# Graph attention edge stages: four buffers of turned one-hots, a ring of ten messages, rounds of turned one-hots and scores at other tiles, both scans for the highest score together

## The reference

```python
xp = (x @ W).reshape(-1, Hh, C)
alpha = a_src[src] + a_dst[dst] + a_edge
alpha = leaky_relu(alpha, 0.2)
m = segment_max(alpha, dst)
ex = exp(alpha - m[dst])
denom = segment_sum(ex, dst)
alpha = ex / (denom[dst] + 1e-16)
out = segment_sum(xp[src] * alpha[:, :, None], dst) + bias
```

## Time and profile before

| what | us |
|---|---|
| median of 3 runs | 3561.06 (3548.32 to 3565.73) |
| profiled execution, its own time | 3566.32 |
| its span, first to last instruction | 3564.4 |
| both edge stages with the join between them | about 140 to 3230 of the span |

### The profile page before, as it was taken

How to read it: one execution, slowest core, us unless ns; L and a number is a source line. 1 busy time by engine, 2 the same in 40 slices (tenths; PEclk the granted TensorE clock), 3 DMA queues, 4 the chain that set the end, 5 groups by cost and what they waited for, 6 DMA issues and landing times. The chain is left out here.

```text
span 3564.4 us, 57920 instructions
## 1 busy us (share of the span) xinstructions
PE 2549.3 (72%) x15613; PEld 2149.2 (60%) x15614; DVE 2146.7 (60%) x6378; ACT 1130.1 (32%) x3915; POOL 2046.6 (57%) x2269
## 2 busy tenths in 40 slices
PE   5376876777777777764777676767676766859897
PEld 4265655655666565644666666656566664648786
DVE  6265666666666665634666665656666666676565
ACT  3133333333333333441222222222222223532222
POOL 3465665565656565365565565656566553636665
PEclk9677777777777777786677776777777767969999
DMA  9544544444444444134444444544444442554443
GB/s 238 168 136 124 139 127 131 132 130 132 133 134 134 132 134 133 50 113 121 136 138 138 137 139 127 146 127 141 134 141 136 138 124 74 166 146 153 141 120 93
DMA packets 282383, 475.56 MB, mean 133 GB/s; under 512 B 69124, under 2 KB 191644, under 8 KB 282116
## 3 DMA queue, kind: packets, MB, share of 16 engines
q0 software_dynamic: 96912, 288.68, 29.9%
q1 hardware_dynamic: 120884, 137.12, 12.5%
q10 hardware_dynamic: 64320, 46.56, 4.2%
HBM read 398.47 MB, written 75.78 MB: 133 GB/s over the span
## 5 line engine op out<-in xcount | busy, mean ns | idle before, releaser
L708 POOL DMA_INDIRECT e_rows<-table,e_idx x1664 | 1610.0, 968 | 1091.9 <-DVE e_msg L749 665.1
L1094 PE MATMUL e_ps_sum<-e_hot,e_msg 128*128 128x128 f32 x6656 | 1196.5, 339 | 251.4 <-DVE e_msg L749 139.4
L1094 PEld LDWEIGHTS e_ps_sum<-e_hot,e_msg 128*128 128x128 f32 x6656 | 1058.0, 242 | 309.0 <-DVE e_msg L749 173.8
L946 ACT ACTIVATE acc<-e_ps_sum 128x256 f32 x1664 | 641.8, 386 | 1574.3 <-remote 929.3
L749 DVE TENSOR_TENSOR e_msg<-e_rows,e_ps_pr 128x256 f32<-128x256 f32 x1664 | 672.2, 416 | 40.3 <-PE e_ps_pr L1085 11.3
L1074 PE MATMUL e_ps_al<-e_dst_score,e_hotT 128*128 x3328 | 331.3, 186 | 376.5 <-issue 209.9
L1074 PEld LDWEIGHTS e_ps_al<-e_dst_score,e_hotT 128*128 128x128 bf16 x3328 | 258.0, 104 | 522.4 <-issue 452.5
L738 DVE TENSOR_SCALAR e_hotT<-e_relb,pcolf 128x512 bf16<-128x512 bf16 x416 | 147.6, 355 | 495.5 <-remote 380.6
L724 DVE TENSOR_TENSOR e_hot<-e_ps_pr,rel 128x508 f32<-128x508 f32 x416 | 283.5, 682 | 0.0
L767 DVE TENSOR_TENSOR e_al<-e_ps_al,e_rows 128x128 f32<-128x128 f32 x104 | 30.3, 292 | 381.5 <-remote 201.4
L2292 ACT ACTIVATE x_h<-x,eb 128x128 f32<-128x128 f32 x216 | 67.9, 366 | 277.9 <-PE x L2366 229.7
(11 more groups left out here) (370 smaller groups left out, 3562.8 us busy)
## 6 DMA issues: line engine op xcount, KB each, us to landing
e_relb<-rel_rows SPq DMA_DIRECT2D x104, 512.0 KB
e_rows<-table,e_idx POOLq DMA_INDIRECT x1664
e_eattr<-in_edge_b SPq DMA_DIRECT2D x104, 128.0 KB
e_xT<-turned_x ACTq DMA_DIRECT2D x100, 128.0 KB
e_xr<-in_x ACTq DMA_DIRECT2D x100, 128.0 KB
node<-l_row SPq DMA_DIRECT2D x25, 512.0 KB, 3.2
table<-t_row SPq DMA_DIRECT2D x25, 276.0 KB
table<-j_row SPq DMA_DIRECT2D x25, 276.0 KB, 2.5
```

The costliest lines, as they stand in the source:

```text
L708: nc.gpsimd.indirect_dma_start(out=rows[q][:, k, :], out_offset=None, in_=table[0:NP], in_offset=bass.IndirectOffsetOnAxis(ap=idx[:, q, k: ...
L946: nc.scalar.activation(acc[:, :, bass.ds(at[k + e], P)], ps_sum[pair % 3][:, e], ACT.Copy).then_inc(s["window"], 1)
L1094: op = nc.tensor.matmul(ps_sum[pair % 3][:, e, a], msg[:, (16 * g + k + e) % RM, a * P:a * P + P], hot[:, (4 * g + k // 4) % RH, (k + e) % ...
```

## The change

`e_hotT` gets four buffers, one for each round, so a round now waits only for the same round of the group before (for r = 3, the `scores` of the group before). The ring of messages shrinks from 14 slots to 10, which frees the same 4 KB of a partition: a message at even k now waits for the pair five back, not seven. DVE makes the rounds at k = 2, 3, 6, 14, and PE uses them at k = 9, 10, 11, 14. `highest` moves from k = 7 to k = 8, straight ahead of `less_highest`.

```diff
-    RM = 14
+    RM = 10
-        hotT = tmp("hotT", [P, 2, 2, 4, P], BF16)
+        hotT = tmp("hotT", [P, 4, 2, 4, P], BF16)
...
                 if r == 0:
                     vec.wait_ge(s[f"rel{q}"], 16 * i + 16)
-                    if g > 0:
-                        vec.wait_ge(s["part"], 3 * g)
-                elif r == 1:
-                    vec.wait_ge(s["scores"], g + 2)
-                else:
-                    vec.wait_ge(s["part"], 3 * g + r - 1)
+                if g > 0:
+                    if r < 3:
+                        vec.wait_ge(s["part"], 3 * g - 2 + r)
+                    else:
+                        vec.wait_ge(s["scores"], g + 2)
...
-                    if ahead and k in (3, 6, 14, 15):
-                        turned_hots(g + 2, q, {3: 0, 6: 1, 14: 2, 15: 3}[k], i + 1)
+                    if ahead and k in (2, 3, 6, 14):
+                        turned_hots(g + 2, q, {2: 0, 3: 1, 6: 2, 14: 3}[k], i + 1)
...
-                    if softmax and k == 7:
+                    if softmax and k == 8:
                         highest(n, p, i if p == 1 else i + 1)
-                    if softmax and k == 8:
                         less_highest(n, p)
...
-                    if ahead and k in (9, 10, 14, 15):
-                        scores(m, q, {9: 0, 10: 1, 14: 2, 15: 3}[k], j)
+                    if ahead and k in (9, 10, 11, 14):
+                        scores(m, q, {9: 0, 10: 1, 11: 2, 14: 3}[k], j)
```

More of the change, by code:

```diff
@@ L730, in turned_hots @@
                     vec.wait_ge(s[f"rel{q}"], 16 * i + 16)
-                    if g > 0:
-                        vec.wait_ge(s["part"], 3 * g)
-                elif r == 1:
-                    vec.wait_ge(s["scores"], g + 2)
-                else:
-                    vec.wait_ge(s["part"], 3 * g + r - 1)
+                if g > 0:
[3 more added lines that the diff above has]
+                        vec.wait_ge(s["scores"], g + 2)
                 for far, number in enumerate((v["pcolf"], v["pfar"])):
-                    op = nc.vector.tensor_scalar(hotT[:, r % 2, far], relb[:, q, 4 * r:4 * r + 4, :], number[:, 0:1], None,
+                    op = nc.vector.tensor_scalar(hotT[:, r, far], relb[:, q, 4 * r:4 * r + 4, :], number[:, 0:1], None,
                                                  ALU.is_equal)
@@ L1073, in scores @@
                     for far in range(2):
-                        op = nc.tensor.matmul(parts_al[:, m, :], hotT[:, r % 2, far, k, :],
+                        op = nc.tensor.matmul(parts_al[:, m, :], hotT[:, r, far, k, :],
                                               pieces[:, bass.ds(b + far, 1), :].rearrange("p a c -> p (a c)"), start=False,
```

## The result

The changed kernel takes 3592.14 us (median of 4 runs, 3585.7 to 3596.23), beside 3558.88 us for the kernel before in the same comparison. The ratio is 1.0094, with a 95% interval of 1.0065 to 1.0124: slower, by about 33 us. Four executions agree within 11 us, so the sign is clear of noise. I had forecast 3522 us and faster. The time is inside the range of 3415 to 3630 us, the direction is wrong.

What follows compares the result with a forecast made beforehand. No engine is full; waits going round between engines, followed through POOL's two gaps, set the time. Per step 0.54 us gained, 0 for gap two, 0.13 lost: 0.41 us, times 100 steps 41 us, so 3522 us; range 3415 to 3630 us.

Steps and rivals of the forecast that it cites:

- The wait on this group's `part` goes, and the stall moves to message 0.: DVE at k = 14 no longer waits; it waits for `probT` at the next step's k = 0, one gather later.
- signs that I had named: One-hots' idle time (about 496 us) nearly gone, `e_msg` idle 300 us or more, `leaky` clearly under 381.5, POOL's waiting about 620.
- wrong, to the bad: Signs of a slower kernel: idle time ahead of `e_peak`, or POOL waiting over 700 us for messages.
- Gap one becomes 1.71 + 0.68 = 2.39 us instead of 2.93.: POOL's stop ahead of DVE's third round: release plus POOL's lag, no round between; 0.54 us less a step.
- I take no change: POOL's stop behind `leaky` keeps its 1.78 us; bounds were all of 1.48 us won and 1.89 us more.
- gap two: POOL's second stop in a step, waiting for the message behind DVE's `leaky`: 1.78 us before the change.
- the scans stand behind a stall: Rival: `turned` comes late, both scans and the subtraction delay message 9; 1.48 us a step slower, 3709 us; chance 0.18.
- Ring of ten: 0.: Message 14 waits for its own group's third pair instead of the first; expected cost 0.
- the ring of ten binds: Rival: DVE stops at k = 14, PE at the sixth pair, a third gap; 0.9 us a step, 3650 us; chance 0.08.
- Rounds inside a run: 0.13 us lost.: DVE's round 2 moves into POOL's run of gathers, lengthening one gather from 0.95 to 1.08 us each step.
- PE's late news is tied to POOL's run, as I read it: All PE signals are held back while POOL gathers back to back, arriving 1.71 us after its run stops.

Runs made afterwards that it cites:

- B: The measuring condition of those comparisons in which the unchanged kernel before takes about 2995 us.
- A: The measuring condition of those comparisons in which the unchanged kernel before takes about 3560 to 3590 us.
- g1: Changed kernel with SP's fetch also waiting for `leaky` of the group two back, on A: 3671.46 us, 1.0243 of the kernel before.
- i1: Changed kernel with SP's fetch also waiting for `leaky` of the group two back, on B: 2971.87 us, 0.9928 of the kernel before.

## Why the prediction was wrong

The time was foreseen as 41 us less and came out as 33 us more. Point by point:

- *The wait on this group's `part` goes, and the stall moves to message 0.* Right, and so were the signs that I had named: 4.1 us ahead of L737, 521.4 us ahead of the messages, and a `leaky` that hardly waits. My signs of "wrong, to the bad" were met too: idle time ahead of `e_peak`, and 728.1 us of POOL's waiting.
- *"Gap one becomes 1.71 + 0.68 = 2.39 us instead of 2.93."* This term failed, and is the larger error: 0.78 us a step between the forecast and the mean of the layers. The place lost 0.01 us in layer 0 and gained 0.48 in layer 1, on average +0.24 instead of -0.54. Of the two addends, the release was met in the step shown (1.67 us), but over 105 waits its mean is 1.90 us (ahead of messages, those over 6 us left out). The other addend I took from the wrong place: POOL starts 1.17 us behind message 0, not 0.68 us as behind messages 15 and 5. I could have read this in the trace of before, where the lag of the first gather of a group has the same mean, 1.2 us. What fills the extra half us no row shows. So the half us that I won by taking a round out of the stall (0.54 us) was lost again, which accounts for a gap that keeps its size. The 0.48 us by which it grew in layer 1 lie at k = 14, where the ring of ten waits. My base was also one short step: 24.92 us, where the mean of the kernel before is 25.7 us in layer 0 and 25.9 us in layer 1.
- *"I take no change"* for gap two. This step failed. It grew by 0.85 us a step in layer 0 and fell by 0.28 us in layer 1, on average +0.29. The mechanism is that of my rival *the scans stand behind a stall*: DVE reached the scans in the silent part of POOL's run in 74 steps, and stood there for 346.6 us. I gave it 0.18 and priced it at 1.89 us for each step. It was met in three steps of four and cost less than that, since the gap in front of it (k = 5, 1.47 and 1.10 us a step before) vanished at the same time. In layer 1 a wait that I didn't count came in front of it, that of `mixed` (64.9 us). I had both halves in the text, for `leaky` 3.9 us earlier means a `turned` in the middle of a run, and took the mean of the bounds instead of following the step on.
- *Ring of ten: 0.* On B it is (0.9993). On A this term was put at nothing wrongly: DVE stood ahead of message 14 for 39 us in 14 steps, and POOL at k = 14 for 0.54 us a step in layer 1. That is the start of my rival *the ring of ten binds*. What it costs in the end isn't shown, since no run on A has the ring alone.
- *Rounds inside a run: 0.13 us lost.* The sign was wrong: gathers became 0.19 us a step shorter in all. A gather beside a round does take longer (1.10 us at 1021.97 beside the round at 1021.64, against 0.95), so the price of one such meeting is right; but before the change three gathers of a step met a round, on average (in layer 0 k = 6, 7 and 15, 1.06 to 1.07 us each), and after it two (k = 5 and 14, 1.03 and 1.04 us). I counted the meeting that was added and not those that went. The rule of the Trainium skill that I had set against this ("SBUF — State Buffer", section "SBUF: two separate sides") agrees in its sign: of that round (1021.64 to 1022.24) 0.27 us lay beside the gather, which took 0.15 us longer. It doesn't speak of how many such meetings the change takes away.
- *PE's late news is tied to POOL's run, as I read it.* Right for this place on A, and too wide as I put it. In all six traces on A DVE goes on 1.3 to 2.2 us after the run, whether it waited at the turned one-hots, at message 0 or at the first scan (means of each such group of more than 50 waits of over 1.5 us that ended behind a run). But news from the first two gathers of a run isn't held back, and of `leaky`'s waits many ended inside a run. In the traces of B, with gathers just as close together, nothing is late. So a run of gathers is not enough for it; the mechanism stays open.
- What I did not look at: SP. Its fetch hangs on `scores`, which the change moves. I counted every wait of DVE and PE and no transfer, and on B that transfer is most of what the change costs.

## What to carry to other kernels

When a stall is removed, don't stop at the next wait: follow the engine on until the work that was late is late again, and price that place by its own rows, for the lag of a consumer isn't the same at each place. A semaphore that moves earlier also releases what hangs on it in the DMA queues; look where those bytes will land, and pin a large prefetch to an event after which nothing urgent is in flight (here after `leaky`: 2.5% of the changed kernel on B). And a schedule tuned in a few tenths of a us is tuned for one condition: the same number of a chip gave A once and B once. Measure the kernel before beside each candidate, and compare ratios only where it takes the same time. Last, when a wait ends with "remote", set the recorded time of the update beside the end of the row that makes it; that settles whether the news or the work is late.

## What the runs showed of the hardware

- The same kernel took 3548 to 3593 us in some comparisons and 2987 to 3003 us in others; two of them, one of each kind, have the same number of a chip. TensorE's mean granted clock (a mean over its levels of 1.2 and 2.4 GHz) was 0.770 of full in the profiled execution of the kernel before on A and 0.843 on B. That is 9%; the clock alone doesn't explain DVE's 495.5 us ahead of the one-hots against 28.6 us.
- On A, what PE signals from the fifth gather of a run on is recorded 4.3 to 4.6 us late (medians; 297 updates), and 0.01 us late while POOL stands still or is in the first two gathers. Where DVE waits for it behind a run, it goes on 1.33 to 2.15 us after the run (means in the changed kernel and g1). On B the updates are 0.01 us late throughout. On B, with no other transfer in the way, the rows of the last gather take 1.89 us (deviation 0.07) to land. That the two are near each other may be chance.
- On B, with a fetch whose first transfer has 512 KB issued 1 to 3 us ahead of the end of a group's last gather, the rows of that group are there 3.57 us (before) and 4.36 us (changed) after that end, instead of 1.89 us (i1).
- 16 gathers of 0.95 us with 0.30 us between them take 20.1 us; plain transfers of as many rows from SP let a step run in 17.1 to 17.2 us (B).
